# Attention of a gated cross-attention block as one float32 product a pair of sequences

## The reference

```
x: 32 x 64 x 512;  ctx: 32 x 64 x 512;  bias: 32 x 32 heads x 64 x 64;  mask: 32 x 64 x 64
q = layernorm(x) @ Wq;  k = ctx @ Wk;  v = ctx @ Wv          # 32 heads of 128
p = softmax(q k^T / sqrt(128) + bias), masked
x = x + tanh(g_xattn) * ((p v) @ Wo)
y = layernorm(x) @ weight^T + bias + LoRA of three adapters by batch
x = x + tanh(g_ffn) * y
```

## Time and profile before

| | |
|---|---|
| median of 3 runs | 1709.41 us (1709.2 to 1711.37) |
| the profiled execution | 1708.84 us |
| its span, first to last instruction | 1707.0 us |
| TensorE busy | 1693.7 us, 8535 products |
| VectorE / ScalarE / GpSimd busy | 944.7 / 701.5 / 901.9 us |
| granted TensorE clock | 1.000 |

### The profile page before, as it was taken

One profiled execution on the slowest core, in us unless ns is written; L12 is line 12 of the kernel. 1 busy time (PEld: TensorE's weight loads), 2 busy tenths in 40 slices (PEclk: granted clock), 3 DMA queues, 4 the chain that ended last, 5 costly groups with the idle time before them and its releaser, 6 DMA issues.

```text
span 1707.0 us, 25377 instructions
## 1 busy us (share of the span) xinstructions
PE 1693.7 (99%) x8535; PEld 1434.5 (84%) x8535; DVE 944.7 (55%) x2136; ACT 701.5 (41%) x1473; POOL 901.9 (53%) x1187
## 2 busy tenths in 40 slices
PE   8999999999999999999999999999999999999998
PEld 7888888888888888888888888888888888888887
DVE  4566555556454454454556566456565655655555
ACT  5555555554344442434333443243333333333331
POOL 5767777765466653654455554454534444334431
PEclk9999999999999999999999999999999999999999
DMA  8877777776677765766778777586766666666541
GB/s 283 293 260 254 276 270 276 272 256 216 217 239 241 249 227 171 247 228 224 249 251 300 271 273 258 161 316 251 264 242 238 213 234 245 235 218 236 210 152 44
DMA packets 162853, 407.94 MB, mean 239 GB/s; under 512 B 15554, under 2 KB 56642, under 8 KB 162724
## 3 DMA queue, kind: packets, MB, share of 16 engines
q1 hardware_dynamic: 162580, 406.05, 68.3%
q10 hardware_dynamic: 144, 0.26, 0.0%
HBM read 313.97 MB, written 92.27 MB: 238 GB/s over the span
## 4 chain that ended last, share of the span: by engine, by line
PE 98%; DVE 1%; ACT 0%; DMA 0%; POOL 0%; issue 0%; DVEq 0%; ACTq 0%
PE vo_bank L395 13%; PE vo_bank L397 13%; PE vo_bank L396 13%; PE q_bank L395 8%; PE q_bank L397 8%; PE q_bank L396 8%; PE k_bank L395 7%; PE k_bank L397 7%; PE k_bank L396 7%; PE s_two L802 7%; PE pv_two L400 5%; PE pv_two L401 2%; PE vo_bank L824 1%; PE vo_bank L835 0%; PE vo_bank L857 0%; PE s_two L395 0%
## 5 line engine op out<-in xcount | busy, mean ns | idle before, releaser
L1508 POOL TENSOR_TENSOR score<-score,row_max 128x256 f32<-128x256 f32 x128 | 78.8, 615 | 513.2 <-DVE row_max L1235 513.2
L1419 POOL TENSOR_TENSOR ot_lo<-attn,ot_hi 128x512 fp32r<-128x512 f32 x128 | 165.9, 1296 | 195.9 <-ACT ot_hi L935 195.9
L1031 ACT ACTIVATE attn<-pv_two 128x512 f32<-128x512 f32 x128 | 76.6, 598 | 416.1 <-PE pv_two L401 416.1
L395 PE MATMUL q_bank<-xt_hi,wq 128*128 128x512 f32 x512 | 208.6, 407 | 0.0
L397 PE MATMUL q_bank<-xt_hi,wq 128*128 128x512 f32 x512 | 200.9, 392 | 0.0
L395 PE MATMUL k_bank<-ct_hi,wk 128*128 128x512 f32 x512 | 199.3, 389 | 1.2 <-DVE ct_lo L1158 1.2
L396 PE MATMUL q_bank<-xt_lo,wq 128*128 128x512 f32 x512 | 200.0, 391 | 0.0
L397 PE MATMUL k_bank<-ct_hi,wk 128*128 128x512 f32 x512 | 199.2, 389 | 0.0
L396 PE MATMUL k_bank<-ct_lo,wk 128*128 128x512 f32 x512 | 199.2, 389 | 0.0
L1207 DVE STREAM_TRANSPOSE pv_two<-score 128x256 f32<-128x256 f32 x128 | 58.8, 460 | 244.5 <-POOL score L1522 242.7
L397 PE MATMUL vo_bank<-wo,ot_lo 128*128 128x512 f32 x496 | 193.0, 389 | 0.0
(11 more groups left out here) (215 smaller groups left out, 3738.0 us busy)
## 6 DMA issues: line engine op xcount, KB each, us to landing
wq<-wq_split SPq DMA_DIRECT2D x96, 512.0 KB, 3.3
wk<-wk_split SPq DMA_DIRECT2D x96, 512.0 KB, 3.8
wo<-wo_split SPq DMA_DIRECT2D x96, 512.0 KB, 5.7
wv<-wv_mixed SPq DMA_DIRECT2D x32, 1024.0 KB, 7.8
wv<-wv_split SPq DMA_DIRECT2D x24, 1024.0 KB, 6.9
raw_bias<-in_pair_bias SPq DMA_DIRECT2D x64, 256.0 KB, 5.8
wq_split<-wq SPq DMA_DIRECT2D x32, 512.0 KB, 2.9
wk_split<-wk SPq DMA_DIRECT2D x32, 512.0 KB, 4.2
```

The costliest lines, as they stand in the source:

```text
L395: pe.matmul(to, left[0], right[0], start=first, stop=False)
L1419: pool.tensor_tensor(to, src, f32(of), ALU.subtract).then_inc(done, 1)
L1508: pool.tensor_tensor(score[:, :, :], score[:, :, :], row_max[:, :].unsqueeze(2).to_broadcast([P, PB, S]), ALU.subtract).then_inc(shift_don ...
```

## The change

- The transposed probabilities are one float32 tile `pt`, written by VectorE's transposes directly (zeros stay in the squares between two sequences). They are not split, nor are the head's values: the attention product is one float32 product a tile, with a slice of `values_f` as its stationary side. ScalarE's `probabilities`, `head_values` and `attention_half`, VectorE's `rest_of_probabilities`, and GpSimd's `head_values` and `attention` are gone.
- Scores and attention each write one whole bank, by turns the first and the second of two. ScalarE rounds the attention's output from the bank to `ot_hi`, and VectorE subtracts to `ot_lo`, in place of its add.
- Semaphores follow: attention waits for the transposes, for the group's values, and for `ot_lo` of two heads before; a place of the value tile is free when the last attention product that reads it has ended (`pv_ps`). `scores` still has, ahead of what the diff shows, its first wait for VectorE's scores of the slot before.
- The ten warm-up products are float32 with 128 columns.
- The statistics of tiles 2 and 3 of the next block are made in slot 28 of a block, not 25.

The diff, cut; left out are declarations of semaphores and the calls of removed functions in the slots and at the end:

```diff
@@ -42,7 +42,7 @@
...
 FFN_SUMS, FFN_PIECES, FFN_TURNS, LORA, DENSE = (5, 6), (7, 8, 11, 12), (9, 10, 13, 14), (14, 17), (17, 18)
-X_LOAD, LEAD_SUMS, LEAD_PIECES, LEAD_TURNS = 20, (22, 25), (19, 20, 24, 25), (25, 26, 29, 30)
+X_LOAD, LEAD_SUMS, LEAD_PIECES, LEAD_TURNS = 20, (22, 28), (19, 20, 24, 25), (25, 26, 29, 30)
 LEAD_CHUNKS = (0, 2, 1, 3)
@@ -285,12 +285,10 @@
...
         values_f = sb("values", [P, V_BLOCKS, 2, G * DH])
-        v = two("v", [P, PB, DH])
         ot = [two(f"ot{i}", [P, BLK]) for i in range(OT_BUFS)]
-        pt = sb("pt", [P, PB, 2, P], F32R)
+        pt = sb("pt", [P, PB, P], F32)
         raw_bias = [sb(f"raw_bias{i}", [P, 2, PB, S]) for i in range(2)]
         score = sb("score", [P, PB, S])
-        attn = sb("attn", [P, BLK])
         kept_gate = sb("kept_gate", [P, BLOCKS * PB])
@@ -324,13 +322,12 @@
...
         vo_bank = [pb(f"vo_bank{i}") for i in range(2)]
-        s_two = ctx.enter_context(nc.psum_tensor("s_two", [P, PB, 2, P], F32))
-        pv_two = ctx.enter_context(nc.psum_tensor("pv_two", [P, PB, 2, P], F32))
+        s_two = ctx.enter_context(nc.psum_tensor("s_two", [P, 2, PB, P], F32))
+        pv_two = ctx.enter_context(nc.psum_tensor("pv_two", [P, 2, PB, P], F32))
         banks = {"q": q_bank, "k": k_bank, "vo0": vo_bank[0], "vo1": vo_bank[1]}
         for i in range(2):
-            banks[f"s{i}"] = s_two[:, 2 * i:2 * i + 2, :, :].rearrange("p a b c -> p (a b c)")
-            banks[f"pv{i}"] = pv_two[:, 2 * i:2 * i + 2, :, :].rearrange("p a b c -> p (a b c)")
-        turned = pv_two[:, 0, :, :].rearrange("p a (c s) -> p (a c) s", s=S)
+            banks[f"s{i}"] = s_two[:, i, :, :].rearrange("p a b -> p (a b)")
+            banks[f"pv{i}"] = pv_two[:, i, :, :].rearrange("p a b -> p (a b)")
@@ -395,10 +392,6 @@
...
             return pe.matmul(to, left[1], right[0], start=False, stop=last)
-
-        def both(pe, to, left, right):
-            pe.matmul(to, left[0], right, start=True, stop=False)
-            return pe.matmul(to[:, 0, :], left[1], right[:, 0], start=False, stop=True)
@@ -797,9 +790,9 @@
...
                 pe.wait_ge(k_out, n + 1)
-                wait(pe, score_done, n)
+                wait(pe, score_done, n - 1)
                 for m in range(PB):
-                    mm = pe.matmul(s_two[:, m, 0, :], qt[:, cols(m, P)], kt[:, m, :], start=True, stop=True)
+                    mm = pe.matmul(s_two[:, n % 2, m, :], qt[:, cols(m, P)], kt[:, m, :], start=True, stop=True)
                 mm.then_inc(s_ps, 1)
@@ -809,11 +802,17 @@
...
                 g, h = divmod(n, G)
-                pe.wait_ge(v_lo, n + 1)
-                pe.wait_ge(pt_lo, n + 1)
-                wait(pe, ot_sum, n)
+                pe.wait_ge(turn_done, n + 1)
+                if g < 2 * FIRST_PAIR:
+                    emptied(pe, ("v", g, PB - 1))
+                elif g % 2 == 0:
+                    emptied(pe, ("w", g // 2, 4, 1))
+                else:
+                    emptied(pe, ("w", g // 2, 5, 1))
+                wait(pe, ot_lo, n - 1)
                 for t in range(PB):
-                    mm = both(pe, pv_two[:, t, :, :], parts(v, slice(None), t, slice(None)), pt[:, t, :, :])
+                    mm = pe.matmul(pv_two[:, n % 2, t, :], values_f[:, v_block(g, t // 2), t % 2, cols(h, DH)], pt[:, t, :],
+                                   start=True, stop=True)
                 mm.then_inc(pv_ps, 1)
@@ -877,10 +876,9 @@
...
-                pe.wait_ge(pt_zero, 2)
+                pe.wait_ge(pt_zero, PB)
                 for _ in range(WARM_UP):
-                    pe.matmul(vo_bank[0][:, :], pt[:, 0, 0, :], pt[:, 0:2, :, :].rearrange("p a b c -> p (a b c)"),
-                              start=True, stop=True)
+                    pe.matmul(vo_bank[0][:, 0:P], pt[:, 0, :], pt[:, 1, :], start=True, stop=True)
@@ -974,22 +972,9 @@
...
                 job = ("v", g, t)
-                wait(act, v_lo, G * (g - V_BLOCKS // 2 + 1))
+                wait(act, pv_ps, G * (g - V_BLOCKS // 2 + 1))
                 act.wait_ge(vo_ps, NUMBER[job] + 1)
                 act.activation(values_f[:, v_block(g, t // 2), t % 2, :], bank_of(job)[:, :], ACT.Copy).then_inc(v_free, 1)
-
-            def head_values(n):
-                g, h = divmod(n, G)
-                wait(act, pv_ps, n)
-                if g < 2 * FIRST_PAIR:
-                    emptied(act, ("v", g, PB - 1))
-                elif g % 2 == 0:
-                    emptied(act, ("w", g // 2, 4, 1))
-                else:
-                    emptied(act, ("w", g // 2, 5, 1))
-                for half in range(2):
-                    last = act.activation(v[0][:, cols(half, 2), :], values_f[:, v_block(g, half), :, cols(h, DH)], ACT.Copy)
-                last.then_inc(v_hi, 1)
@@ -1002,7 +987,7 @@
...
                     if p == 1:
-                        act.wait_ge(v_lo, V_READ[g, half])
+                        act.wait_ge(pv_ps, V_READ[g, half])
                         act.wait_ge(vo_ps, NUMBER["w", u, 1, t] + 1)
@@ -1015,26 +1000,11 @@
...
-            def probabilities(n):
-                if n == 0:
-                    act.wait_ge(pt_zero, PB)
-                wait(act, pv_ps, n)
-                act.wait_ge(turn_done, n + 1)
-                for r in range(2):
-                    rows = cols(r, S)
-                    last = act.activation(pt[rows, :, 0, rows], turned[rows, :, :], ACT.Copy)
-                last.then_inc(pt_hi, 1)
-
-            def attention_half(n):
-                wait(act, ot_lo, n)
-                act.wait_ge(pv_ps, n + 1)
-                act.activation(by(attn, PB), pv_two[:, :, 1, :], ACT.Copy).then_inc(ot_b, 1)
-
             def attention(n):
...
                     act.wait_ge(vo_ps, NUMBER["o", (n - OT_BUFS) // G, PB - 1] + 1)
-                act.wait_ge(ot_sum, n + 1)
-                hi(ot[n % OT_BUFS][0][:, :], attn[:, :], ot_hi)
+                act.wait_ge(pv_ps, n + 1)
+                hi(ot[n % OT_BUFS][0][:, :], banks[f"pv{n % 2}"][:, :], ot_hi)
@@ -1095,10 +1062,8 @@
...
                 if n > 0:
-                    attention_half(n - 1)
+                    attention(n - 1)
                 exps(n)
-                if n > 0:
-                    attention(n - 1)
                 if in_next(n) == n - 1:
@@ -1194,7 +1156,7 @@
...
                             if p in (2, 6, 4):
-                                dve.wait_ge(v_lo, V_READ[to])
+                                dve.wait_ge(pv_ps, V_READ[to])
                             last = dve.tensor_tensor(values_f[:, v_block(*to), t, :], bank_of(("w", u, p, t))[:, :],
@@ -1202,23 +1164,19 @@
...
                 if n == 0:
-                    emptied(dve, ("v", 0, PB - 1))
+                    dve.wait_ge(pt_zero, PB)
+                wait(dve, pv_ps, n)
                 dve.wait_ge(prob_done, n + 1)
-                dve.transpose(turned[:, :, :], score[:, :, :]).then_inc(square_done, 1)
+                for a in range(2):
+                    rows = cols(a, S)
+                    last = dve.transpose(pt[rows, :, rows], score[rows, :, :])
+                last.then_inc(square_done, 1)
                 dve.wait_ge(square_done, n + 1)
...
                         of, to = cols(2 * a + i, S // 2), cols(2 * a + 1 - i, S // 2)
-                        last = dve.transpose(turned[to, :, cols(i, S // 2)], score[of, :, cols(1 - i, S // 2)])
+                        last = dve.transpose(pt[to, :, cols(2 * a + i, S // 2)], score[of, :, cols(1 - i, S // 2)])
                 last.then_inc(turn_done, 1)
-
-            def rest_of_probabilities(n):
-                dve.wait_ge(pt_hi, n + 1)
-                for r in range(2):
-                    rows = cols(r, S)
-                    last = dve.tensor_tensor(pt[rows, :, 1, rows], turned[rows, :, :], f32(pt[rows, :, 0, rows]),
-                                             ALU.subtract)
-                last.then_inc(pt_lo, 1)
@@ -1227,7 +1185,7 @@
...
                     rows = cols(a, S)
-                    last = dve.scalar_tensor_tensor(out=score[rows, :, :], in0=s_two[rows, :, 0, rows],
+                    last = dve.scalar_tensor_tensor(out=score[rows, :, :], in0=s_two[rows, n % 2, :, rows],
                                                     scalar=SCALE, in1=raw_bias[m % 2][rows, n % 2, :, :],
@@ -1235,8 +1193,8 @@
...
             def attention(n):
-                dve.wait_ge(ot_b, n + 1)
-                dve.tensor_tensor(by(attn, PB), pv_two[:, :, 0, :], by(attn, PB), ALU.add).then_inc(ot_sum, 1)
+                dve.wait_ge(ot_hi, n + 1)
+                lo(ot[n % OT_BUFS][1][:, :], banks[f"pv{n % 2}"][:, :], ot[n % OT_BUFS][0][:, :], ot_lo)
@@ -1360,7 +1317,7 @@
...
             for t in range(PB):
-                dve.memset(f32(pt[:, t, :, :]), 0.0).then_inc(pt_zero, 1)
+                dve.memset(pt[:, t, :], 0.0).then_inc(pt_zero, 1)
             dve.wait_ge(wk_hi, 1)
@@ -1471,14 +1427,6 @@
...
-            def head_values(n):
```

(33 more changed lines are left out.)

## The result

| | before | after |
|---|---|---|
| median | 1709.31 us (6 runs, 1708.58 to 1711.37) | 1697.27 us (6 runs, 1696.88 to 1697.9) |
| span of the profiled execution | 1707.0 us | 1695.5 us |
| first score block starts at | 23.77 us | 24.29 us |
| score block of slots 4 and 24 | 71.12, 326.18 | 70.00, 323.60 |
| a plain slot | 12.753 us | 12.680 us |

The ratio is 0.993, 95% interval 0.9918 to 0.9941. The gain is 12.0 us in the medians and 11.5 us in the two profiled spans. The forecast was 9.1 us and 1700.3 us with a low end of 1698.0: the direction and the named waits held, the size did not.

What follows compares the result with a forecast made beforehand. TensorE, busy 1693.7 of 1707.0 us, was taken as the bound. 4.5 us from attention products plus 4.56 us of waits gave 9.1 us saved, 1700.3 us; the range was 1698.0 to 1704.9.

Steps and rivals of the forecast that it cites:

- the named waits: TensorE stalls in slots 1, 2, 25 and 57 and at the end go: 1.14 + 0.32 + 2.0 + 1.1 = 4.56 us.
- The bound: TensorE, busy 1693.7 of 1707.0 us, bounds the kernel; other engines' work counts only where TensorE waits for it.
- The stalls in slots 1, 2, 25 and 57: TensorE's waits for low-half probabilities (1.14 and 0.32 us) and for VectorE emptying the output bank (2.0 us together) go.
- The tail: Last group's output projections stop waiting for the attention output's low half: stalls of 0.63 and 0.47 us go, 1.1 us.
- What was costed at nothing: Added waits, longer-held values, SBUF transposes, work moved to VectorE, GpSimd's moved deviations and the changed warm-up cost 0 us.
- The attention product: Float32 attention block takes the score block's 0.902 us instead of 0.942: 0.035 x 128 slots = 4.5 us saved.
- a second reading: Plain slots: scores and attention together cost 1.823 us, becoming 2 x 0.902 = 1.804, a saving of 0.02 a slot.
- The first: Rival: attention block keeps its length, loads or whatever both forms share set the pace; only waits go, 1704.8 us; 13%.
- No wait came back: Rival: TensorE arrives 1 to 3 us earlier at DMA-brought weights and waits; only the product term remains, 1704.9 us; 8%.
- values read in place: Rival: attention loads from the shared value tile stand in the open, 0.08 us four times a slot, 41 us: 1741; 4%.

Runs made afterwards that it cites:

- the run with the old block apart: Kernel before with its attention block moved behind the first three query products of the next slot: 1708.70 us, ratio 0.9996.
- eight short float32r products: Changed kernel with each float32 attention product replaced by two float32r products of 128 columns on context data, attention's result left out: 1702.35 us, ratio 0.9961.
- behind four: Changed kernel with each float32 attention product replaced by one float32r product of 128 columns, attention's result left out: 1643.88 us in a single run.

## Why the forecast was right and where it failed

- *The bound.* Right. TensorE stayed at 99%, and 648 us less work on three engines counts only through the named stalls.
- *The stalls in slots 1, 2, 25 and 57.* Right: 1.46 + 2.0 forecast, 1.34 + 2.08 measured. Slot 89 had a smaller one of 0.13, which I had passed over.
- *The tail.* 1.1 forecast, 1.5 measured. I priced a stall by the distance to the next start alone; the step behind it is long too (0.31 and 0.34 us instead of 0.23, behind the products at 1666.43 and 1678.39 of the earlier trace rows), and the last attention block is shorter. Mechanism right, size low.
- *What was costed at nothing* (longer-held values, waits on the transposes, the subtraction on VectorE, deviations on GpSimd, the warm-up). Nothing of it shows as a releaser of TensorE in a slot. One releaser is new: a wait of 0.32 us at 9.96 us for weights that GpSimd splits (`wv`), ahead of the first scores. It stands in six of the nine profiles of the changed kernel and its variants and in none of the three of the kernel before; whether the change causes it was not tried. The 0.52 us by which the first score block starts late in the profile of after is no cost of the change that I can show: in the other runs built on the changed kernel it starts between 23.59 and 24.18, and in those built on the kernel before between 23.73 and 23.91.
- *The attention product: here it failed.* The term was 4.5 us with bounds 2.6 and 5.1; it measured 7.0. The price of the block standing apart was right: 0.035 taken, 0.0335 measured. The step that failed is the one from there to all 128 slots. I had taken the price in a slot where the blocks are apart and multiplied it by 128, though 97 slots have them touching, where the difference is 0.073. I had a second reading made in touching slots, which should have warned me, and it came out at 0.02 for a wrong reason: its step of 0.2277 us was averaged from the third 512-column product on, and the first dozen behind the old block are slow. In slot 4 of the kernel before the 13th such product starts at 75.71 and the 48th at 83.64; 35 steps of 0.2266:

```profile
72.88 0.46 PE L395 MATMUL q_bank<-xt_hi,wq 128*128 128x512 f32 x1
...
75.71 0.39 PE L395 MATMUL k_bank<-ct_hi,wk 128*128 128x512 f32 x1
...
83.64 0.39 PE L397 MATMUL vo_bank<-wo,ot_lo 128*128 128x512 f32 x1
```

With 0.2266 scores and attention cost 12.753 - 48 x 0.2266 = 1.876, not 1.823, and the scores alone 2.04 - 5 x 0.2266 = 0.907. That is a saving of 1.876 - 2 x 0.907 = 0.062, and with the 0.013 that two float32 blocks save where they touch it is 0.075, near the measured 0.073. An error of 0.001 us in a step was multiplied by 48 steps and 128 slots: 6 us. The 1.876 are not all spent in the blocks: the slow products behind them are in it, and there lay most of the saving. I had even argued that this reading counted something twice and leaned to the lower price, with bounds of 0.02 and 0.04 of which neither came from the right rate.
- *From 0.073 to 7.0.* 97 x 0.073 + 31 x 0.0335 is 8.1. The rest of about 1 us is given back in slots where a transposed input stands directly ahead of the scores. There three float32 blocks follow one another, and the first twelve 512-column steps behind them take 2.847 us on average over 19 such slots (2.808 before), against 2.820 behind scores and attention alone (2.832 before): (0.039 + 0.012) x 19 = 1.0.
- *Rivals.* The first had the loads set the pace, and the new block's loads do follow one another at a fixed 0.112 us; but the old block took 0.03 more for its eight, and the products behind it were slow, so its 1704.8 did not come. No wait came back in the slots (the DMA engines are as busy as before), and values read in place cost nothing visible: L814 and L795 differ by 1 ns. The range failed at its low end, which I had set by the forecast's own bounds and one microsecond.

The order with scores and attention always next to one another, 1696.63 us, is below both kernels. Its interval overlaps that of the change. In its profile slots 25 to 127 are 0.46 us shorter (1313.55 against 1314.01), so it is an improvement of about half a microsecond at most.

## What to carry to other kernels

On an engine that is 99% busy the gain is in the price of its own blocks: take a step's price from products that have settled, count what the block does to the products behind it as part of its price, and multiply only within slots where the neighbours are the same. Count instructions before columns when products are short. Before moving a step to cure a stall, ask whether another part of the same change already cures it.

## What the runs showed of the hardware

- A float32r product of 128 columns costs 0.112 us beside 0.227 for 512 columns: half the time for a quarter of the columns. The float32 product of 128 columns costs 0.22 us, as much as two such.
- The products behind a block belong to its price. Twelve 512-column products take 2.72 us at the settled rate. Behind a float32 block they take 2.82, nearly all of it in the first step. Behind the old attention block they take 2.83 where it follows the scores directly (78 slots) and 2.79 where it stands apart (31 slots, and 2.79 again in the run with the old block apart). Behind eight short float32r products they take 2.83 in both places, behind four 2.83 and 2.79. In the slow cases about ten steps start late. Since eight and four products of 128 columns in banks by turns show it too, neither columns of 256 and 128 by turns nor the shared bank is needed for it; what decides was not settled.
- The old attention block (256 and 128 columns by turns) next to a float32 block costs 0.027 us more than apart; two float32 blocks next to one another cost 0.013 us less.
